# First group's keys 0 to 2, queries 0 and values 0 loaded in the projection's last chunk, and the ones rows written by DMA

## The reference, cut to what matters

```
q, k, v = split(x @ Wqkv)                      # x: 4096 x 512, Wqkv: 512 x 1536
q = layernorm(q) * q_scale ; k = layernorm(k) * k_scale
16 heads of 32: p = softmax(causal(q / sqrt(32) @ k^T)) ; ctx = p @ v
x = layernorm(x + ctx @ out_W)
gate, up, down: int32 weights -> (w - 128) * scale, 512 -> 2048 -> 512
x = layernorm(x + down(silu(gate(x)) * up(x)))
```

## Time and profile before

| | |
|---|---|
| median of 3 runs | 2434.85 us (2434.4 to 2436.08) |
| profiled execution, its time | 2433.1 us |
| its span, first to last instruction | 2431.4 us |
| busy in the span | PE 96%, DVE 74%, ACT 54%, POOL 11% |
| mean granted PE clock | 0.981 |

### The profile page before, as it was taken

The page is one execution under the profiler, slowest core; times in us unless marked ns, Lnnn a source line. Parts: engine busy times, 40 slices in busy tenths (PEclk is TensorE's granted clock), DMA queues, the critical chain, the costliest instruction groups (busy, mean ns, idle before and its releaser), DMA issues. The chain is left out here.

```text
span 2431.4 us, 34396 instructions
## 1 busy us (share of the span) xinstructions
PE 2329.9 (96%) x12546; PEld 1405.1 (58%) x12546; DVE 1787.6 (74%) x1833; ACT 1315.8 (54%) x1631; POOL 268.1 (11%) x266
## 2 busy tenths in 40 slices
PE   8999966999999999999999999959999999999997
PEld 7888832433343333433334333348888888888885
DVE  7777764989979899798997989944555565565654
ACT  4444555888888888888888888801111111111111
POOL 1111111111031110311103111000000000000000
PEclk9999978999999999999999999979999999999999
DMA  7777684010730106301063010091111121110100
GB/s 247 256 242 251 233 217 94 23 32 6 140 84 23 32 6 137 87 23 32 6 136 88 23 32 6 6 298 50 31 55 36 35 70 35 36 52 18 35 18 18
DMA packets 126388, 197.27 MB, mean 81 GB/s; under 512 B 14992, under 2 KB 39568, under 8 KB 126224
## 3 DMA queue, kind: packets, MB, share of 16 engines
q1 hardware_dynamic: 126224, 195.10, 28.7%
HBM read 122.70 MB, written 72.35 MB: 80 GB/s over the span
## 5 line engine op out<-in xcount | busy, mean ns | idle before, releaser
L884 ACT ACTIVATE probs<-score 128x1024 f32<-128x1024 f32 (+3 forms) x1152 | 1024.5, 957 | 212.1 <-PE score L802 190.9
L950 DVE TENSOR_TENSOR total<-total,probs 128x2048 f32<-128x2048 f32 (+3 forms) x472 | 983.0, 2083 | 78.3 <-POOL probs L763 33.8
L802 PE MATMUL score<-qstk,kstk 98*128 98x512 f32 (+3 forms) x2304 | 656.5, 407 | 38.1 <-DMA qstk<-shift 21.5
L802 PEld LDWEIGHTS score<-qstk,kstk 98*128 98x128 f32 x2304 | 377.0, 189 | 528.8 <-ACT probs L884 410.2
L818 PE MATMUL ctx_acc<-probs,values 128*32 128x512 f32 (+3 forms) x4608 | 575.1, 571 | 8.3 <-POOL probs L763 8.0
L1289 ACT ACTIVATE hidden<-slot,gate_scale_sb 128x512 f32<-128x512 f32 x128 | 88.1, 688 | 624.8 <-PE slot L1218 624.7
L763 POOL TENSOR_SCALAR_AFFINE_SELECT probs<-probs 128x512 f32<-128x512 f32 x128 | 190.1, 1486 | 1032.1 <-ACT probs L884 1032.1
L1374 DVE SCALAR_TENSOR_TENSOR hidden<-slot,up_scale_sb,hidden 128x512 f32<-128x512 f32 x128 | 96.0, 750 | 262.2 <-ACT hidden L1289 262.2
L818 PEld LDWEIGHTS ctx_acc<-probs,values 128*32 128x32 f32 x4608 | 92.0, 108 | 201.6 <-issue 161.2
L1218 PE MATMUL slot<-xt_hi,wg_sb 128*128 128x512 f32 x512 | 201.5, 394 | 6.0 <-issue 6.0
L1229 PE MATMUL y<-wd_sb,h_hi 128*128 128x512 f32 x512 | 199.4, 389 | 1.4 <-DVE h_lo L1382 1.4
(11 more groups left out here) (101 smaller groups left out, 1984.1 us busy)
## 6 DMA issues: line engine op xcount, KB each, us to landing
qstk<-q_hi SPq DMA_DIRECT2D x64, 256.0 KB
kstk<-k_hi SPq DMA_DIRECT2D x64, 256.0 KB, 9.5
wq_int<-in_wq SPq DMA_DIRECT2D x48, 256.0 KB, 3.2
wq_float<-wq_f SPq DMA_DIRECT2D x48, 256.0 KB, 2.7
x_raw<-in_x_t SPq DMA_DIRECT2D x32, 256.0 KB, 3.6
v_rows<-v_out SPq DMA_DIRECT2D x32, 256.0 KB, 2.3
q_hi<-part_hi SPq DMA_DIRECT2D x32, 256.0 KB, 2.3
q_lo<-part_lo SPq DMA_DIRECT2D x32, 256.0 KB, 2.6
```

The costliest lines, as they stand in the source:

```text
L802: ins = pe.matmul(score[u % RING][:, i, cut(t):], kstk[0:ROWS, h, kb * P:(kb + 1) * P], qstk[0:ROWS, q_buffer[ch], h, cut(t):], start=True ...
L884: act.activation(probs[:, t % PB, 2 * p:2 * p + 2, cut(t):], score[u % RING][:, :, cut(t):], ACT.Exp).then_inc(exped, 1)
L950: dve.tensor_tensor(into, into, now, ALU.add).then_inc(added, 1)
```

## The change

- `keys`, `queries` and `first_values` are allocated around both blocks. `keys` is laid out by chunk, so that chunks 0 to 2 take the 24 KiB that `w_raw` has in `project`; `queries` 0 takes the place of `ow_raw`. `x_raw`, `x_hi`, `x_lo`, `wq_int`, `wq_f` and `part_hi` lie on other parts of them.
- In the last chunk, SP loads keys 0, ones rows 0, queries 0 and values 0 after unit 1 (nine DMAs), keys and ones rows 1 after unit 3, and keys and ones rows 2 after unit 5 (four DMAs each).
- Ones rows come from a DRAM tensor `one_rows`, stored once at the start; the eight memsets are gone. Keys 3 to 7 of group 0 get their ones rows by a small DMA each.
- `zeros` is a quarter as large, and `shift` is written by four DMAs. ACT's split of `ow_raw` moves to unit 4 of the first chunk, and POOL's becomes four pieces in the first chunk's third and fourth row tiles.
- In group 0 of `attend`, SP waits for all stores, then loads queries 1, values 1, queries 2, values 2, then keys and values 3 to 7, and from queries 3 on as before.

```diff
+def key_load(sp, dr, keep, g, j, s):
+    for r, src in enumerate(("k_hi", "k_lo", "k_hi")):
+        sp.dma_start(keep["keys"][r * HD:(r + 1) * HD, j, :, :].bitcast(F32), ...).then_inc(s, 16)
+def one_load(sp, dr, keep, j, s):
+    sp.dma_start(keep["keys"][3 * HD:ROWS, j, :, :].bitcast(F32), dr["one_rows"].rearrange("a (h s) -> a h s", h=HG)).then_inc(s, 16)
...
-            sp.dma_start(dr["shift"].rearrange("a h (u s) -> (a h u) s", u=4), zeros[:]).then_inc(zero_stored, 16)
+            for u in range(4):
+                sp.dma_start(dr["shift"].rearrange("a h (p u s) -> u (a h p) s", u=4, p=4)[u], zeros[:]).then_inc(zero_stored, 16)
+            sp.dma_start(dr["one_rows"].rearrange("a (h s) -> (a h) s", h=HG), one_fill[:]).then_inc(zero_stored, 16)
...
+                    if not after and u in (1, 3, 5):
+                        ahead(u // 2)
+            def ahead(j):
+                if j == 0:
+                    sp.wait_ge(w_low_done, 3 * DC)
+                    sp.wait_ge(zero_stored, 80)
+                    for one in parts_stored:
+                        sp.wait_ge(one, 32 + 64 * AHEAD)
+                    for one in v_stored:
+                        sp.wait_ge(one, 16 + 32)
+                    sp.wait_ge(fin_pool, 1 + NG)
+                key_load(sp, dr, keep, 0, j, keep["k_in"][j])
+                one_load(sp, dr, keep, j, keep["k_in"][j])
+                if j == 0:
+                    query_load(sp, dr, keep, 0, 0, 0, keep["q_in"][0])
+                    value_load(sp, dr, keep["first_values"][:], 0, 0, keep["v_in"][0])
...
+            for st in range(ST):
+                root(0, st, 0)
+                root(0, st, 1)
+                for g in range(NG // 2 * (st - 2), NG // 2 * (st - 1)) if st > 1 else ():
+                    pool.wait_ge(ow_high, 1)
+                    pool.tensor_tensor(ow_lo[:, g, :], ow_raw[:, g, :], ow_hi[:, g, :].bitcast(F32), ALU.subtract).then_inc(fin_pool, 1)
+            with pool.Fori(1, NCH) as n:
...
-            pool.tensor_tensor(ow_lo[:], ow_raw[:], ow_hi[:].bitcast(F32), ALU.subtract).then_inc(fin_pool, 1)
...
-                if not after:
-                    act.wait_ge(ow_in, 16)
-                    act.activation(ow_hi[:], ow_raw[:], ACT.Copy).then_inc(ow_high, 1)
+                    if not before and u == 4:
+                        act.wait_ge(ow_in, 16)
+                        act.activation(ow_hi[:], ow_raw[:], ACT.Copy).then_inc(ow_high, 1)
...
-                if before is None:
-                    stored(1)
-                load("q", 0)
-                load("kv", 0)
                 if before is None:
                     stored(NCH)
-                load("q", 1)
-                for j in range(1, NCH):
-                    load("kv", j)
+                    load("q", 1)
+                    load("kv", 1)
+                    load("q", 2)
+                    for j in range(2, NCH):
+                        load("kv", j)
...
-            for j in range(NCH):
-                dve.memset(kstk[3 * HD:P, :, j * CH:(j + 1) * CH].bitcast(F32), 1.0).then_inc(ones_ready, 1)
```

More of the change, by code:

```diff
@@ L623, in attend, with value @@
         g_full = probs[:, 0, 2, 0:P]
[L625 to L638, removed]
+        def value(kb):
+            return keep["first_values"][:, kb, :] if kb < ST else values[:, kb - ST, :]
         def store(eng, g, ch):
@@ L685, in _ @@
                     sp.nop(nofuse=True)
+                for j in range(AHEAD):
+                    key_load(sp, dr, keep, 0, j, g_again)
+                query_load(sp, dr, keep, 0, 0, 0, g_again)
             def group(g, before):
@@ L703, in load @@
[L703 to L706, removed]
-                if before is None:
-                    stored(1)
-                load("q", 0)
-                load("kv", 0)
+                    if before is not None or j >= AHEAD:
+                        end = key_end[j] + 1 - NS
+                        sp.wait_ge(scored, 2 * NS * g + 2 * end + Q_CREDIT)
+                        sp.nop(nofuse=True)
+                        key_load(sp, dr, keep, g, j, k_in[j])
+                        if before is None:
+                            one_load(sp, dr, keep, j, k_in[j])
+                        sp.wait_ge(valued, NS * g + end + V_CREDIT)
+                        sp.nop(nofuse=True)
@@ L711, in group @@
+                    to = values[:, (j - 1) * ST:j * ST, :] if j else keep["first_values"][:]
+                    value_load(sp, dr, to, g, j, v_in[j])
                 if before is None:
                     stored(NCH)
-                load("q", 1)
-                for j in range(1, NCH):
-                    load("kv", j)
-                if before is not None:
+                    load("q", 1)
[3 more added lines that the diff above has]
+                        load("kv", j)
+                else:
+                    load("q", 0)
+                    load("kv", 0)
+                    load("q", 1)
+                    for j in range(1, NCH):
+                        load("kv", j)
@@ L717, in group @@
                     store(sp, before, NCH - 1)
                 for ch in range(2, NCH):
-                    load("q", ch)
+                    if before is not None or ch > 2:
+                        load("q", ch)
                     store(sp, g, ch - 2)
@@ L801, in scores @@
                         h = 2 * p + i
-                        ins = pe.matmul(score[u % RING][:, i, cut(t):], kstk[0:ROWS, h, kb * P:(kb + 1) * P],
-                                        qstk[0:ROWS, q_buffer[ch], h, cut(t):], start=True, stop=True)
+                        ins = pe.matmul(score[u % RING][:, i, cut(t):], keys[0:ROWS, kb // ST, h, kb % ST * P:(kb % ST + 1) * P],
+                                        queries[0:ROWS, q_buffer[ch], h, cut(t):], start=True, stop=True)
                     ins.then_inc(scored, 1)
@@ L1461, in build @@
         }
-        project(nc, io, dr, keep)
-        attend(nc, io, dr, keep)
+        base = (nc.sbuf_base + 31) // 32 * 32
+        with ExitStack() as both:
+            keep["keys"] = both.enter_context(nc.sbuf_tensor("keys", [P, NCH, HG, CH], F32R))
+            keep["queries"] = both.enter_context(nc.sbuf_tensor("queries", [P, 3, HG, CH], F32R))
+            keep["first_values"] = both.enter_context(nc.sbuf_tensor("first_values", [P, ST, P], F32))
+            keep.update(keys_at=base, queries_at=base + 64 * KIB)
+            project(nc, io, dr, keep)
+            attend(nc, io, dr, keep)
         finish(nc, io, dr, keep)
```

90 lines of the change are left out of this document (56 added, 34 removed).

## The result

| | before | changed |
|---|---|---|
| median | 2435.22 us (2434.4 to 2436.08, 4 runs) | 2413.26 us (2409.09 to 2414.25, 4 runs) |
| profiled execution, its span | 2433.1, 2431.4 us | 2409.09, 2407.3 us |

The ratio is 0.9911, with a 95% interval of 0.9898 to 0.9923. The change made the kernel faster by 22 us, where 29 were forecast: the sign is right, and the median is 7.3 us over the forecast and 1.3 us outside the range. The profiled execution was the fastest of the four.

The account below looks back on a forecast made before the run. The prediction took the kernel as bound by the chain through PE and, in attention, the Exp feeding it. 10.4 + 24.2 - 5.7 = 28.9 us off 2433.1 gave 2404.2 profiled, 2406.0 for the median, range 2400.0 to 2412.0.

Parts of the forecast that it names:

- The first gap: PE idle before attend's first scores until keys 0 arrive; loading them early was to gain 10.4 us.
- The second gap: PE idle from 363.34 to 384.83 until queries 2 arrive; issuing them third was to gain 24.2 us.
- The slip: Early loads delay the stores in the projection's last chunk, so its end comes 5.7 us later.
- The engines' work: DMA engines' time for the early loads in the projection's last chunk, priced at 16.4 us.
- 16.4 - 7.6 - 3.1: Projection's last chunk: DMA work less free engine time less the stores' leeway before ACT reuses the buffer, giving 5.7 us.
- Two-row transfers: Three ones-row and one shift transfer on two engines each: 2 us more delay by the skill's rule, not in the forecast.
- Queries 3: Last load of attend's early burst: there after 42 us, wanted 48 us after the first scores, priced at nothing.
- the rival of a new wait: Queries 1 or 3 arrive after chunk 1 or 3 of attend wants them: 2409 to 2413 us, chance 0.13.
- The chip's pace in chunk 0 I leave as it is: Attend's chunk 0 keeps 8.85 us from first mask to first mask, starting at the 1.2 GHz clock in either kernel.
- everything after it waits for attention, so a microsecond taken from either gap is one off the end: Time saved at the seam between projection and attention was to reach the kernel's end in full.
- The sum: Whole kernel: 10.4 + 24.2 - 5.7 = 28.9 us off the profiled 2433.1, giving 2404.2 us.
- The early loads' own worth: At the seam: 10.4 us gained before the first scores less 5.7 us lost in the projection, 4.7 us.

Follow-up runs that it names:

- e2_order: The kernel before with queries 2 issued after keys and values 1, and no early loads: 2412.93 us, ratio 0.9916.
- e3_one: The changed kernel with only keys 0, queries 0 and values 0 loaded early (9 DMAs): 2411.88 us, ratio 0.9911.
- e8_memset: The changed kernel with the ones rows of keys 0 to 2 set by three DVE memsets, not early two-row DMAs: 2410.92 us, ratio 0.9909.
- e13_back31: The changed kernel with 62 always-met waits in PE's skipped attend branch, putting finish's branch target back at instruction 25354: 2407.36 us, ratio 0.9893.

## Why the prediction was right or wrong

- **The first gap** (10.4 us): right. Flag to first score fell from 15.89 to 5.59 us, 10.3.
- **The second gap** (24.2 us): right in a profiled execution with a quick clock. Chunk 1 to chunk 3 fell by 24.14 us; in the three with a long slow stretch it fell by 21 to 22. The order alone made the median 21 us lower (e2_order), with a slow stretch of 21 us in its profile.
- **The slip** (5.7 us): near in size, and in part by luck. The flag is late by 6.65, 5.54, 6.4, 7.2 and 7.1 us in the five profiles of the changed program, 6.6 in the mean; with only keys, queries and values 0 it is 3.2. The engines' work was priced well: from 268 to 329 their share rises from 0.64 to 0.89, which is 15.3 us, for 3.25 MB more (13.90 to 17.15), where 16.4 us were forecast and the rate of the earlier trace rows was taken. But the step from this work to the slip, 16.4 - 7.6 - 3.1, leaves out SP's time for issuing, which delayed a job's stores by some 3 us. By the same step e3_one was expected at 322.5 to 323.5, and it was 325.65. So the 5.7 came out near 6.6 without this term, and how the slip divides stays open.
- **Two-row transfers.** By the rule of the Trainium skill quoted in the prediction ("DMA: Bandwidth & Descriptors", section "Why a DMA increments its semaphore by 16 and not by 1"), the slip would be 7.7 us, and 1.5 to 2 less without the ones rows. e8_memset's is 7.8 without three of the four transfers, but it holds a stop of 2.04 us that its memsets brought. So no run here shows what they cost, nor that they cost nothing.
- **Queries 3** (6 us to spare): they had none, 0.30 us late in one profile, and some 1.5 in e2_order and e3_one. The burst moved 194 GB/s from 334 to 383.5, not 208, and SP issued the stores of chunk 0 ahead of them (366.24 to 368.40), which the 8.2 MB left out. Queries 1 and chunk 1 had no wait, so the rival of a new wait did not come true, but only just.
- **What failed: two terms taken as nothing.** The first is the slow clock. "The chip's pace in chunk 0 I leave as it is", and chunk 1 to chunk 2 was priced by group 1's 15.58 us, where the clock is full. The slow stretch of before's profile was a short one of 9 us; it is 9 to 21, and the wait that covered its end was the one removed. Over the five profiles of the changed program chunk 0's pace is 9.2 us in place of 8.85, and chunk 1 to chunk 2 is 17.2 in place of 15.58 (15.2 with a quick clock, 17.8 to 19.0 with a late one). The second is finish. The step "everything after it waits for attention, so a microsecond taken from either gap is one off the end" took the time after attend as fixed. The change does not edit finish, but the waits taken out of PE's program moved finish's code by 31 instructions: first gate to first down matmul takes 13.8 to 14.9 us with the stop and 10.1 to 10.7 without.
- **The sum.** The five profiled executions of the changed program took 2412.5 us in the mean, where the sum gave 2404.2: 8.3 over. Slip 6.6 - 5.7 = 0.9; flag to first score 5.8 - 5.5 = 0.3; first score to chunk 2's first mask 29.8 - 27.8 = 2.0, the slow clock; chunk 3's first mask to POOL's first mask in finish (L1215) 1173.8 against 1172.8 us, 1.0; first gate to first down matmul 14.2 against 10.1, 4.1. Together 8.3. The 1.0 us in attend stay unexplained. With the code back in its place the change gives 2407.36 us (e13_back31), 1.4 us from the forecast of 2406.0; by the stop alone it would be some 3 us more, so this closeness owes something to chance.
- **The early loads' own worth**, 10.4 - 5.7 = 4.7 us by the prediction, is 2412.93 - 2407.36 = 5.6 us between two kernels that both lack the stop (by the ratios to before, 0.9916 - 0.9893 of 2434, also 5.6). The two intervals just overlap, but each of the four runs of e13_back31 is below each of the five of e2_order. That e2_order tied with the whole change says nothing of the early loads: the stop takes some 4 of these 5.6 us back, and the rest is within the scatter of the runs.

## What to carry to other kernels

When a wait is removed, ask what varying thing ran beneath it, and price the new path by several executions, not by one. A change that adds or removes instructions ahead of a taken branch moves the code behind it, even if that code is not edited: look for a stop without a releaser soon after the branch, and move the target past the start of a piece. When one experiment puts work on another engine, as e8_memset does, look in its trace for what that work holds up before reading its time. Look into the compiled program before you believe in a pad, and before you read two equal times (here e2_order's and the change's) as proof that a part is worth nothing.

## What the runs showed of the hardware

- A taken branch over skipped code took PE some 3.6 us in one place and 6.3 in the other. In each, one packet of the instruction queue lands (330.5 to 332, 1594 to 1598), so the time is read as that of bringing the instructions in. Sequencer rows of the changed kernel at attend's and at finish's start, with the DMA engines nearly idle at the first and full at the second:

```profile
L832 PEldq COMPARE_BRANCH  x1: 3597/3597/3597, 330.5 to 330.5; - x1
...
L1319 PEldq COMPARE_BRANCH  x1: 6280/6280/6280, 1591.7 to 1591.7; - x1
```

  The Trainium skill, "Advanced Engine Details and Errata", section "Control Flow Timing", gives some 108 ns for a compare-and-branch; these take 33 and 58 times that.
- If the target lies some 20 instructions ahead of the end of a piece, a second stop of 3.2 to 3.5 us follows; the DMA queues were full there in these traces, and what it would be without that was not tried. With the target 10 instructions into a piece there is none. The stop came before the sixth matmul, each of two instructions (weights and matmul), after about 13 of the 21 counted, so the pieces seem to begin some 8 instructions ahead of the multiples of 256 in the compiled file; that offset was not tested further.
- PE's clock after a standstill came back after 9 to 21 us of unbroken work in executions of the same program. What decides it was not found.
